# First settling stage of a two-layer graph network: TensorE turns the next tile's rows between a tile's two products, VectorE normalises two tiles ahead

## The reference

```python
def gatv2(x, src, dst, Ws, bs, Wd, bd, attn):
    fs = (x @ Ws + bs).reshape(-1, H, D)
    fd = (x @ Wd + bd).reshape(-1, H, D)
    e = leaky_relu(fs[src] + fd[dst], 0.2)
    ...                                   # softmax over the edges of a node
    out = segment_sum(alpha[:, :, None] * fs[src], dst)
    return elu(out)
h = gatv2(x, src, dst, W1s, b1s, W1d, b1d, attn1)      # 8 heads
h = layer_norm(h + x, ln1_w, ln1_b)                    # the stage of this change ...
out = gatv2(h, src, dst, Wos, bos, Wod, bod, attno)    # ... makes this fs and fd too; 1 head
return layer_norm(out, lno_w, lno_b)
```

## Time and profile before

| | us |
|---|---|
| time before, median of 3 runs | 3361.42 (3357.31 to 3370.45) |
| the profiled execution, its own time | 3364.68 |
| span of its profile | 3363.0 |
| from the barrier ahead of the first settling to its last matmul | about 909 to 1102.1 |
| ten tiles of products in it, first to last matmul | 927.36 to 1102.12 |

### The profile page before, as it was taken

One profiled execution on the slowest core, in us unless ns is written; L12 is line 12 of the kernel. 1 busy time (PEld: TensorE's weight loads), 2 busy tenths in 40 slices (PEclk: granted clock), 3 DMA queues, 4 the chain that ended last, 5 costly groups with the idle time before them and its releaser, 6 DMA issues. The chain is left out here.

```text
span 3363.0 us, 59697 instructions
## 1 busy us (share of the span) xinstructions
PE 2863.0 (85%) x13556; PEld 2142.5 (64%) x13557; DVE 2307.4 (69%) x4380; ACT 1689.3 (50%) x5352; POOL 1623.9 (48%) x2067
## 2 busy tenths in 40 slices
PE   5885888888699799998777999999999976777699
PEld 3442444445355455554347999999999874555598
DVE  6536889889766788887575555555555447888743
ACT  0004889889622133332334665656566566777400
POOL 4666666566456555553113555454554445555201
PEclk9897999999999899999788999999999998999899
DMA  4235344444511565555218777777777747666412
GB/s 140 83 82 159 118 133 132 118 133 134 166 38 48 162 170 171 171 171 167 76 63 267 246 240 241 244 238 241 242 242 226 226 142 224 199 213 206 122 34 65
DMA packets 175009, 546.00 MB, mean 162 GB/s; under 512 B 55332, under 2 KB 56344, under 8 KB 174724
## 3 DMA queue, kind: packets, MB, share of 16 engines
q0 software_dynamic: 82000, 370.33, 35.2%
q1 hardware_dynamic: 70596, 122.50, 11.6%
q10 hardware_dynamic: 22304, 52.11, 5.0%
HBM read 461.31 MB, written 83.81 MB: 162 GB/s over the span
## 5 line engine op out<-in xcount | busy, mean ns | idle before, releaser
L2195 PE MATMUL pO<-wh,gT 128*128 128x384 f32 x3264 | 866.1, 339 | 13.2 <-ACT gT L2146 12.0
L805 POOL DMA_INDIRECT row<-fs_d,rec x400 | 456.0, 1140 | 385.2 <-PE pA L1330 159.5
L2195 PEld LDWEIGHTS pO<-wh,gT 128*128 128x128 f32 x3264 | 593.4, 188 | 21.4 <-ACT gT L2146 19.4
L2195 PE MATMUL pO<-wl,gT 128*128 128x384 f32 x1632 | 546.8, 335 | 0.0
L2209 DVE TENSOR_SCALAR cntge<-pT 128x768 int32<-128x768 int32 x137 | 131.2, 958 | 423.4 <-ACT gT L2146 217.1
L1038 ACT ACTIVATE sj<-sj 128x96 f32<-128x96 f32 x1176 | 313.0, 268 | 78.4 <-DVE sj L1155 77.6
L2146 ACT ACTIVATE gT<-cntge 128x256 fp32r<-128x256 f32 x822 | 294.2, 410 | 29.4 <-DVE cntge L2212 4.5
L2195 PEld LDWEIGHTS pO<-wl,gT 128*128 128x128 f32 x1632 | 307.8, 189 | 0.0
L805 POOL DMA_INDIRECT row<-y_d,rec x200 | 203.4, 1017 | 173.7 <-PE pR L2341 115.9
L1077 PE MATMUL pS<-row,ident 128*128 128x384 f32 x400 | 175.8, 523 | 129.3 <-DVE sj L1155 80.6
L2341 PE MATMUL pR<-row,share 128*128 128x384 f32 x384 | 164.3, 580 | 118.4 <-issue 72.9
(11 more groups left out here) (386 smaller groups left out, 5998.1 us busy)
## 6 DMA issues: line engine op xcount, KB each, us to landing
fdt<-in_L_gnn_W_rel_dram SPq DMA_DIRECT2D x170, 384.0 KB
startrow<-seen_d ACTq DMA_DIRECT2D x141, 320.0 KB
raw<-in_L_gnn_W_rel_dram SPq DMA_DIRECT2D x34, 384.0 KB
row<-fs_d,rec POOLq DMA_INDIRECT x400
kept_d<-fdt SPq DMA_DIRECT2D x10, 384.0 KB
kept<-kept_d SPq DMA_DIRECT2D x10, 384.0 KB
fs_d<-of SPq DMA_DIRECT2D x9, 388.0 KB
fd_d<-of SPq DMA_DIRECT2D x9, 388.0 KB
```

The source lines that it names most:

```text
L805: pool.indirect_dma_start(b["row"][u][:, j, :].bitcast(words), None, table, bass.IndirectOffsetOnAxis(ap=b["rec"][u][:, 2 * j + field:2 * ...
L2195: last = pe.matmul(pO[:, q, 0:HALF], gT[:, c, half, :].bitcast(F32R), w[:, c, lo:up].bitcast(F32R), start=c == 0 and k == 0, stop=c == KC ...
```

## The change

Within the first settling, the arithmetic and the number of instructions on PE, DVE and ACT stay as they are; their order moves.

- PE: the turning of tile t+1 stands between the two half products of tile t. The wait for Wod stands once, ahead of the first product.
- DVE: tiles 0 and 1 are normalised first; then, for each tile t up to 7, the evacuation of the first half, the normalisation of tile t+2, the evacuation of the second half. `step` is cut into `norm`, `first` and `second`. The last two tiles have evacuations alone.
- ACT: `Exp` and `Sqrt` of tile t+2 behind the copy of `pT` of tile t+1.
- POOL: the gathers of tiles 0 and 1 are issued at the start, and that of t+2 in the turn of tile t, once its `y` has been written; the last two tiles are written out behind the loop.

```diff
@@ PE @@
-                        step(pe, 0, 0, True)
+                        turn(0, 0)
                         pe.wait_ge(ahead.w_in, 16)
+                        pe.wait_ge(w_in, 16)
                         with pe.Fori(0, 4) as i:
-                            step(pe, i, 0, False)
-                            step(pe, i, 1, True)
-                            step(pe, i, 1, False)
-                            step(pe, i + 1, 0, True)
-                        step(pe, 4, 0, False)
-                        step(pe, 4, 1, True)
-                        step(pe, 4, 1, False)
+                            half(i, 0, 0)
+                            turn(i, 1)
+                            half(i, 0, 1)
+                            half(i, 1, 0)
+                            turn(i + 1, 0)
+                            half(i, 1, 1)
+                        half(4, 0, 0)
+                        turn(4, 1)
+                        half(4, 0, 1)
+                        half(4, 1, 0)
+                        half(4, 1, 1)
@@ DVE @@
-                        twice(step, dve)
+                        norm(0, 0)
+                        norm(0, 1)
+                        with dve.Fori(0, 4) as i:
+                            for b in range(2):
+                                first(i, b)
+                                norm(i + 1, b)
+                                second(i, b)
+                        for b in range(2):
+                            first(4, b)
+                            second(4, b)
@@ ACT @@
-                        twice(step, act)
+                        norm(0, 0)
+                        turned(0, 0)
+                        norm(0, 1)
+                        with act.Fori(0, 4) as i:
+                            turned(i, 1)
+                            norm(i + 1, 0)
+                            turned(i + 1, 0)
+                            norm(i + 1, 1)
+                        turned(4, 1)
@@ POOL @@
-                        fetch(0)
-                        COPIES = 6
-                        with pool.Fori(0, NT // 2) as i:
+                        for b in range(2):
+                            fetch(b)
...
+                        with pool.Fori(0, NT // 2 - 1) as i:
                             for b in range(2):
-                                n = COPIES // 2 * b
-
-                                y_ok.wait(pool, i, b - 1)
-                                pool.wait_ge(hg_in[1 - b], i * 16 + 16 * b)
+
+                                y_ok.wait(pool, i, b)
                                 pool.sem_inc(posted, 1)
-                                pool.tensor_copy(gindex[1 - b][:], permc[:, ds(i * 2 + (b + 1), 1)]).then_inc(copied, 1)
+                                pool.tensor_copy(gindex[b][:], permc[:, ds(i * 2 + (b + 2), 1)]).then_inc(copied, 1)
...
-                                fetch(1 - b)
+                                fetch(b)
```

More of the change, by code:

```diff
@@ L1485, in settle_first @@
                 prod_ok, evac_ok, fd_ok = (Signal(st, n, 2, 2, 2) for n in ("prod_ok", "evac_ok", "fd_ok"))
[L1487 to L1497, removed]
                 with nc.Block() as block:
@@ L1560, in _, with norm, turned @@
                             s.open(act)
[L1562 to L1570, removed]
-                        twice(step, act)
+                        def norm(i, b):
+                            low_ok.wait(act, i, b)
+                            act.activation(low[:], low[:], ACT.Exp).then_inc(exp_ok.sem, 1)
+                            var_ok.wait(act, i, b)
+                            act.activation(mv[:, 2:3], mv[:, 1:2], ACT.Sqrt).then_inc(root_ok.sem, 1)
+                        def turned(i, b):
+                            t_ok.wait(act, i, b)
+                            prod_ok.wait(act, i, b - 2)
+                            act.activation(split(hT[b][:]), halves(pT), ACT.Copy).then_inc(hT_ok.sem, 1)
+                        norm(0, 0)
[7 more added lines that the diff above has]
+                        turned(4, 1)
                     @block.tensor
@@ L1577, in _, with turn, half @@
                             s.open(pe)
[L1579 to L1590, removed]
-                        step(pe, 0, 0, True)
+                        def turn(i, b):
+                            h_ok.wait(pe, i, b)
+                            hT_ok.wait(pe, i, b - 1)
+                            pe_transpose(pe, pT, ht[b], P).then_inc(t_ok.sem, 1)
+                        def half(i, b, w):
+                            hT_ok.wait(pe, i, b)
+                            evac_ok.wait(pe, i, b - 1, w + 1)
+                            pe_product(pe, pO[w], hT[b], wt[w], P).then_inc(prod_ok.sem, 1)
+                        turn(0, 0)
                         pe.wait_ge(ahead.w_in, 16)
+                        pe.wait_ge(w_in, 16)
                         with pe.Fori(0, 4) as i:
-                            step(pe, i, 0, False)
-                            step(pe, i, 1, True)
-                            step(pe, i, 1, False)
-                            step(pe, i + 1, 0, True)
-                        step(pe, 4, 0, False)
-                        step(pe, 4, 1, True)
-                        step(pe, 4, 1, False)
+                            half(i, 0, 0)
[9 more added lines that the diff above has]
+                        half(4, 1, 1)
                     @block.vector
@@ L1646, in step, with first @@
+                        def first(i, b):
                             v = Steps(dve, dve4b, i * 8 + b * 4)
@@ L1653, in step, with second @@
                             dve.sem_inc(evac_ok.sem, 1)
+                            assert v.n == 2, v.n
+                        def second(i, b):
+                            v = Steps(dve, dve4b, i * 8 + (b * 4 + 2))
                             prod_ok.wait(dve, i, b, 2)
```

97 lines of the change are left out of this document (52 added, 45 removed).

## The result

The changed kernel took 3356.8 us and the kernel before 3364.62, medians of ten runs each; the ratio is 0.9966 with a 95% interval from 0.9954 to 0.9977, that is 11.4 us less. One of the ten runs of the changed kernel took 10016.31 us at a granted clock of 0.273, and it is left out of the ratio; the other nine have a median of 3356.12. The forecast was 12.0 us less. Two further groups of runs gave 0.9969 (0.9954 to 0.9984) and 0.9949 (0.9931 to 0.9967). The gain is real, 0.3 to 0.5%; all three intervals stay clear of 1, so a gain of this size can be told from no change here, which the prediction doubted. The absolute number, 3349.4, was too low by 6.7 us against the nine runs: 3.2 of it because the median of the kernel before came out higher in ten runs than in the three shown, and 3.5 because the two medians are 8.5 us apart and not 12.0.

The account below looks back on a forecast made before the run. TensorE was taken as the bound, waiting only for the copy of `pT`; -12.4 (chain) + 0.3 (head) + 0.1 (drift) = -12.0 us, from a median of 3361.4 to 3349.4 us, range 3341 to 3358.

Parts of the forecast that it names:

- TensorE's chain: First settling, first product to last matmul: 9.95 + 139.3 + 7.9 + 5.2 = 162.4 us, 12.4 us less than before.
- The head stays as it is: Start of the stage: first gather's delay costs 0.3 us, the earlier wait for Wod nothing, first product at 927.36 as before.
- the drift: VectorE falling behind TensorE over seven tiles: 7 x (16.1 - 16.06) = 0.3 us, counted as 0.1 us in the sum.
- the slack: VectorE's second evacuation reads its PSUM tile at T + 14.5, TensorE wants it at T + 16.6: 2.1 us to spare.
- the cycle: VectorE's time per tile in the new order: 15.9 to 16.4 us, taken as 16.1.
- the hand-over added for the new order: One more VectorE hand-over per tile not hidden in a wait; hand-overs cost 0.34 to 0.76 us.
- the tie that was feared: VectorE's 16.1 us per tile against TensorE's 16.06, harmless only if there is slack.
- 1 us to spare: ScalarE's Exp of tile t+2 waits for VectorE and not the reverse, with 1 us to spare.
- VectorE as the bound: Rival: VectorE's cycle outruns TensorE's by more than the slack; 3358 us at worst; chance 0.14 shared with a head loss.
- The late gather: Rival: each normalisation waits 3.18 us for its gather before `y`, time 3370 us; chance 0.04 shared with other losses.
- Nothing gained: Rival: TensorE's 1.06 us wait reappears ahead of the turn or second half, time 3361 us; chance 0.02.
- Faster by over 0.5%: Rival: spread of the runs or a change in a later stage brings 3344 us or less; chance 0.08.

Follow-up runs that it names:

- the useless matmuls: Matmuls of no use put ahead of the first turn of the changed kernel: ratio to the kernel before 0.9964 with 20, 0.9968 with 24.

## Why the prediction was right, point by point

- **TensorE's chain: right.** 162.4 us forecast; 164.0, 162.7 and 162.8 in three profiles. The turn was put at 0.58 from the relational products and is 0.65 (936.24 to 936.89), nine times 0.07. The half products have their 7.74. What is left over in the first profile is the first half, 10.90 instead of 9.95.
- **The head stays as it is: right, with some luck.** The sum had 0.3 us of loss here; from the start of the stage to the first product it is 18.6 to 18.7 us in the three profiles against 18.74 before. The wait for the gather moved by nothing (3.21 against 3.18). Wod still had 3 us to spare. The term of the first half product was taken from one row as if it were constant, and it varies by 1.3 us between runs of the same kernel, more than the head and the drift that the sum priced.
- **VectorE: the slack right, the cycle too long.** The slack of 2.1 us is in the rows (950.93 to 953.03). The cycle is about 15.7 us, not 16.1. The term that was mis-sized is the hand-over added for the new order: the sum put 0.3 to 0.8 us on 15.6, and about 0.1 of it can be seen. The hand-over behind a normalisation is 0.22 us (the 948.98 row) where it was 0.34, which pays for part of the new one; the rest was not taken apart. So the tie that was feared, 16.1 against 16.06, is a margin of 0.4 to 0.5, the drift of 0.1 us in the sum is none, and the slack is never used. The result doesn't hang on it.
- **ScalarE: right.** In the changed kernel the copy, the load and the Exp of the third tile stand at

```profile
937.18 0.81 ACT L1571 ACTIVATE hT<-pT 128x768 f32<-128x768 f32 x1 [5.83 <-PE pT L163]
938.01 1.28 ACT L1564 ACT_TABLE_LOAD   x1
940.64 0.84 ACT L1564 ACTIVATE low<-low 128x768 f32<-128x768 f32 x1 [1.35 <-DVEq L1637]
```

  The Exp waited 1.35 us for VectorE, where 1 us to spare was forecast. Where it did not have to wait, at 945.93 to 947.23 in the run with VectorE's order alone, the Exp started 1.30 us behind the table load's start: the drain that the Trainium skill adds in "ScalarE: Activation LUTs" ("What ACT_TABLE_LOAD costs") isn't there either. One correction to the part on the change: ScalarE's own sequence is the same in both kernels (Exp and Sqrt of a tile, copy, and so on); what moved is when VectorE and TensorE ask for each.
- **The rivals.** VectorE as the bound: did not happen, and the form of its price was borne out: 7 x (cycle - 16.14) less the slack that is left gives 2.8 and 10.3 us, measured 2.9 and 10.7. The late gather: did not happen; the only wait for `hg` is the first. Nothing gained: did not happen; TensorE waits nowhere in the loop. Faster by over 0.5%: 0.9966 in the comparison above; one later group gave 0.9949, with an interval (0.9931 to 0.9967) that reaches to both sides of 0.5%.

## What to carry to other kernels

Where a single-buffered copy between two steps of one engine leaves a gap, put independent work of that engine between them; but the feeding engine must then be that much further ahead, and the two reorderings here are a pair: TensorE's alone cost 49 us in the stage, and VectorE's alone 41.5, or 5.7 with ScalarE's queue moved to suit, where together they save 11. How near a second engine is to being the bound can be measured by adding known instructions until the wait appears, since the sum of hand-overs was off by some 0.4 us in a margin of 0.4 to 0.5; but an instruction added between the two ends of the slack shortens the slack as well as lengthening the cycle, and the expectation has to count it twice. Before speeding up the start of a pipeline, see who else was working beside the slow part: the cold first product was nearly hidden, and removing it won about 1 us of 3.

## What the runs showed of the hardware

- A pause of TensorE can cost more than its length. With 5.5 to 5.8 us of pause in each 23.7, every turn behind one ran at the length it has at the lower clock (1.54 against 0.82) and the product was 0.95 to 1.40 us longer, mean granted clock 0.87.
- The length of the pause does not settle it in these runs. Of eight pauses of 3.39 to 3.76 us, six were followed by a product of 9.60 to 10.66 us and two, of 3.39 and 3.41, by one of 8.01. In the run with ScalarE reordered too, a gap of 1.92 us was followed by a product of 9.69, and one of 1.93 by one of 8.00. The same pause of 2.59 us stands ahead of the useless matmuls in four profiles; they ran at a granted clock of 1.00 in three, and at 0.64 up to 912 in the fourth. A pause of 2.58 us behind them was followed by a turn of 1.54 us and a window at 0.56; a pause of 3.0 us with a turn shortly ahead of it was followed by a product at full speed (8.00), and its window shows 1.00:

```profile
922.00:927.00 5.00, 2.00 (x11) 1.28 (x10) 2.15 (x4) 3.40 (x4) 4.09 (x4) 1.00 0.96 314
```

- The first half product behind 18 us of idleness took from 9.59 to 10.90 us to the next start in profiles of one and the same kernel; in the longest, the granted clock was 0.50 from 925.3 to 930 and 0.88 from there to 936.2. So the time until the clock rises is not the same each time.
- A gather of 384 KB beside 3.5 MB of loads took 9.1 us from its issue to the instruction that waits for it (907.53 to 916.65 in the changed kernel). With the loads held back it had landed 3.9 us after its issue (910.20, and SyncE, which waits for it, went on at 914.13), and VectorE's wait of 3.2 us was gone.
